# A two-layer graph kernel on one core: W_lang is loaded first, in four transfers, and TensorE's first product stands ahead of layer 0

## The reference, cut to what matters

```python
x = _layernorm(x + _L0_gnn_ref(x, adj, adj, L0_gnn_bias), axis=-1)
x = _layernorm(x + _L1_gnn_ref(x, adj, W_lang, W_grav, W_V, W_O, gate_logit, log_sigma), axis=-1)

# L0: W = adj * adj; out = einsum('bnf,nm->bmf', x, W) + bias
# L1:
z_l = einsum('bnd,ed->bne', h, W_lang); z_g = einsum('bnd,ed->bne', h, W_grav)
v = einsum('bnd,ed->bne', h, W_V)
zn = z_l / max(norm(z_l), EPS)
A_l = max(zn @ zn.T, 0) * not_eye
A_g = exp(-d2(z_g) / (2 sigma^2)) * not_eye
K = w_l * rows_normalised(A_l * adj) + (1 - w_l) * rows_normalised(A_g * adj)
out = (K @ v) @ W_O.T
```

## Time and profile before

| | us |
|---|---|
| median of 3 runs (lowest, highest) | 684.94 (684.61, 684.97) |
| the profiled execution, whole | 685.29 |
| its span, from first to last instruction | 683.5 |
| PE busy | 669.0 (98%) |
| PEld busy | 571.0 (84%) |
| DVE busy | 532.2 (78%) |
| ACT busy | 345.6 (51%) |
| POOL busy | 210.4 (31%) |

### The profile page before, as it was taken

The page is one execution under the profiler, slowest core; times in us unless marked ns, Lnnn a source line. Parts: engine busy times, 40 slices in busy tenths (PEclk is TensorE's granted clock), DMA queues, the critical chain, the costliest instruction groups (busy, mean ns, idle before and its releaser), DMA issues.

```text
span 683.5 us, 11745 instructions
## 1 busy us (share of the span) xinstructions
PE 669.0 (98%) x3579; PEld 571.0 (84%) x3579; DVE 532.2 (78%) x1523; ACT 345.6 (51%) x614; POOL 210.4 (31%) x454
## 2 busy tenths in 40 slices
PE   7999999999999999999999999999999999999994
PEld 6888888888888888888888888888888888888883
DVE  5935697878879787887968787796978779697786
ACT  4734445464454546455454645545474554545433
POOL 0222315051341515134151513416051331503022
PEclk9999999999999999999999999999999999999998
DMA  7201102011110201111020111102011110001002
GB/s 280 107 7 57 61 32 94 1 62 63 56 68 31 92 0 61 61 61 61 31 92 0 64 59 61 61 31 92 0 66 57 61 61 31 32 0 63 1 31 94
DMA packets 20406, 38.33 MB, mean 56 GB/s; under 512 B 1824, under 2 KB 1824, under 8 KB 20384
## 3 DMA queue, kind: packets, MB, share of 16 engines
q1 hardware_dynamic: 20384, 38.05, 15.3%
HBM read 21.27 MB, written 16.78 MB: 56 GB/s over the span
## 4 chain that ended last, share of the span: by engine, by line
PE 92%; DVE 3%; ACT 2%; DMA 1%; issue 1%; POOL 1%; SPq 0%; POOLq 0%; DVEq 0%
PE ring L357 56%; PE bank_p L377 12%; PE ring L475 4%; PE bank_x L318 3%; PE bank_p L318 3%; PE bank_k L421 3%; PE bank_r L421 3%; PE bank_pt L390 2%; PE bank_r L397 1%; DMA w_raw<-in_L_gnn_W_lang_dram 1%; PE bank_pt L336 1%; PE bank_r L336 1%; PE bank_k L336 1%; PE bank_pt L408 1%; PE bank_x L336 1%
## 5 line engine op out<-in xcount | busy, mean ns | idle before, releaser
L562 ACT ACTIVATE yT_hi<-ring 128x512 fp32r<-128x512 f32 x128 | 75.9, 593 | 113.5 <-PE ring L357 113.3
L357 PE MATMUL ring<-hT_hi,T_hi 128*128 128x512 f32 x320 | 130.5, 408 | 0.6 <-DVE hT_lo L772 0.5
L357 PE MATMUL ring<-hT_hi,T_lo 128*128 128x512 f32 x320 | 125.4, 392 | 0.0
L357 PE MATMUL ring<-hT_lo,T_hi 128*128 128x512 f32 x320 | 124.7, 390 | 0.0
L777 DVE TENSOR_TENSOR yT_lo<-ring,yT_hi 128x512 fp32r<-128x512 f32 x128 | 87.5, 684 | 35.3 <-ACT yT_hi L562 35.3
L357 PE MATMUL ring<-M_hi,hT_hi 128*128 128x512 f32 x256 | 101.5, 396 | 0.0
L357 PE MATMUL ring<-M_hi,hT_lo 128*128 128x512 f32 x256 | 100.2, 391 | 0.0
L357 PE MATMUL ring<-M_lo,hT_hi 128*128 128x512 f32 x256 | 99.9, 390 | 0.0
L1084 POOL TENSOR_SCALAR z_ve<-z_mv 128x2 f32<-128x2 f32 x32 | 7.0, 218 | 268.8 <-DVE z_mv L873 264.1
L1077 POOL TENSOR_TENSOR x_lo<-x_sb,x_hi 128x512 fp32r<-128x512 f32 x60 | 76.4, 1301 | 22.4 <-ACT x_hi L562 22.4
L614 ACT ACTIVATE o_sb<-o_sb,z_nb,z_rs 128x512 f32<-128x512 f32 x60 | 47.2, 810 | 62.3 <-POOL z_nb L1089 62.3
(11 more groups left out here) (159 smaller groups left out, 1390.6 us busy)
## 6 DMA issues: line engine op xcount, KB each, us to landing
x_sb<-in_x_dram SPq DMA_DIRECT2D x15, 1024.0 KB, 5.2
out_dram<-o_sb SPq DMA_DIRECT2D x60, 256.0 KB, 2.0
x_sb<-in_x_dram SPq DMA_DIRECT2D x2, 512.0 KB, 5.5
w_raw<-in_L_gnn_W_lang_dram SPq DMA_DIRECT2D x1, 1024.0 KB, 6.7
o_sb<-in_L_gnn_W_grav_dram SPq DMA_DIRECT2D x1, 1024.0 KB, 9.4
h_sb<-in_L_gnn_W_V_dram SPq DMA_DIRECT2D x1, 1024.0 KB, 11.6
w_raw<-in_L_gnn_W_O_dram SPq DMA_DIRECT2D x1, 1024.0 KB, 7.9
out_dram<-x_sb SPq DMA_DIRECT2D x4, 256.0 KB, 2.0
```

What stands on the lines that cost most here:

```text
L357: last = pe.matmul(bank[:, :], a, b, start=n == 0, stop=n == len(terms) - 1)
L562: return act.activation(dst, src, ACT.Copy, scale=scale)
```

## The change

SP loads W_lang first, in four DMAs of 128 rows with a semaphore each; adj, all of x (two DMAs), bias, gates, W_grav and W_V follow. TensorE does 21 warm-up transposes in place of 27; its block rows of L come first, then layer 0 of pairs 0 and 1, then row 0 of G, layer 0 of pairs 2 and 3, and rows 1 to 3 of G. ACT splits W_lang ahead of all of x, and its `hi_row`s and `hi_weight`s are put in another order. DVE splits W_lang ahead of the mix and takes out L row 0 ahead of splitting x.

```diff
-    WARM_UP = 27
+    WARM_UP = 21
+        w0_loaded = [sem(f"w0_loaded{c}") for c in range(DC)]
...
-            sp.dma_start(x_sb[:, 0:2, :], x_v[0][:, 0:2, :]).then_inc(x0_loaded[0], 16)
+            for c in range(DC):
+                sp.dma_start(w_raw[0][:, c, :], w_lang[c * R:(c + 1) * R, :]).then_inc(w0_loaded[c], 16)
             sp.wait_ge(adj_zeroed, 1)
             for b in range(2):
                 s = slice(b * N, (b + 1) * N)
                 sp.dma_start(adj_bd[s, s], adj).then_inc(adj_loaded, 16)
-            sp.dma_start(w_raw[0][:, :, :], w_lang.rearrange("(c p) d -> p c d", p=R)).then_inc(w_loaded[0], 16)
+            for c in range(2):
+                s = slice(2 * c, 2 * c + 2)
+                sp.dma_start(x_sb[:, s, :], x_v[0][:, s, :]).then_inc(x0_loaded[c], 16)
             sp.dma_start(bias_bc[:, :], bias.partition_broadcast(R)).then_inc(bias_loaded, 16)
-            sp.dma_start(x_sb[:, 2:4, :], x_v[0][:, 2:4, :]).then_inc(x0_loaded[1], 16)
...
-            pe.wait_ge(mix_steps, 5)
             for s in (L, G):
-                layer0(0, 2 * s)
-                layer0(0, 2 * s + 1)
                 for i in range(DC):
                     setup(...)
+                    if s == G and i == 0:
+                        layer0(0, 2)
+                        layer0(0, 3)
+                if s == L:
+                    pe.wait_ge(mix_steps, 5)
+                    layer0(0, 0)
+                    layer0(0, 1)
...
             def hi_weight(i):
-                act.wait_ge(w_loaded[i], 16)
+                if i:
+                    act.wait_ge(w_loaded[i], 16)
                 for c in range(DC):
+                    if i == 0:
+                        act.wait_ge(w0_loaded[c], 16)
...
+            hi_weight(0)
             split_x0(0)
-            hi_weight(0)
             split_x0(1)
 
             act.wait_ge(gates_loaded, 32)
...
             hi_row(L, 0)
+            hi_row(L, 1)
             hi_weight(1)
-            for i in range(1, DC):
-                hi_row(L, i)
+            hi_row(L, 2)
+            hi_row(L, 3)
+            hi_weight(2)
+            hi_row(G, 0)
             normalise_h(0, 0, 0)
             normalise_h(0, 0, 1)
-            hi_weight(2)
-            for i in range(DC):
-                hi_row(G, i)
-                if i >= 2:
-                    normalise_h(0, 0, i)
+            hi_row(G, 1)
+            hi_row(G, 2)
+            hi_row(G, 3)
+            normalise_h(0, 0, 2)
+            normalise_h(0, 0, 3)
...
-            dve.wait_ge(adj_loaded, 32)
-            (the four operations of mix)
...
-            split_x0(0)
-            dve.tensor_tensor(mask[:, :], adj_bd[:, :], off_diag[:, :], ALU.mult).then_inc(mix_steps, 1)
             lo_weight(0, 0, DC)
+            dve.wait_ge(adj_loaded, 32)
+            (the four operations of mix)
+            lo_row(L, 0)
+            split_x0(0)
+            lo_row(L, 1)
+            lo_weight(1, 0, DC)
+            lo_row(L, 2)
             split_x0(1)
             dve.wait_ge(bias_loaded, 16)
             add_y(0, 0, 0)
-            lo_row(L, 0)
+            lo_row(L, 3)
+            dve.tensor_tensor(mask[:, :], adj_bd[:, :], off_diag[:, :], ALU.mult).then_inc(mix_steps, 1)
             count_y(0, 0, 0)
-            lo_weight(1, 0, 2)
-            lo_row(L, 1)
-            lo_weight(1, 2, DC)
-            lo_row(L, 2)
-            lo_row(L, 3)
 
             dve.wait_ge(gate_exp, 1)
...
             dve.wait_ge(gate_steps, 3)
+            lo_row(G, 0)
             add_y(0, 0, 1)
             count_y(0, 0, 1)
             for i in range(DC):
-                lo_row(G, i)
+                if i:
+                    lo_row(G, i)
                 lo_weight(2, i, i + 1)
```

More of the change, by code:

```diff
@@ L966, in split_x0 @@
                     dve.tensor_tensor(x_lo[:, p, :], x_sb[:, p, :], x_hi[:, p, :], ALU.subtract).then_inc(x_lo_done, 1)
+            lo_weight(0, 0, DC)
+            dve.wait_ge(adj_loaded, 32)
+            dve.tensor_tensor(mix[:, :], adj_bd[:, :], adj_bd[:, :], ALU.mult).then_inc(mix_steps, 1)
+            dve.wait_ge(mix_steps, 2)
+            dve.tensor_tensor(mix[:, :], mix[:, :], ident[:, :], ALU.add).then_inc(mix_steps, 1)
+            dve.wait_ge(mix_steps, 3)
+            dve.tensor_copy(mix_hi[:, :], mix[:, :]).then_inc(mix_steps, 1)
+            dve.wait_ge(mix_steps, 4)
+            dve.tensor_tensor(mix_lo[:, :], mix[:, :], mix_hi[:, :], ALU.subtract).then_inc(mix_steps, 1)
+            lo_row(L, 0)
             split_x0(0)
-            dve.tensor_tensor(mask[:, :], adj_bd[:, :], off_diag[:, :], ALU.mult).then_inc(mix_steps, 1)
-            lo_weight(0, 0, DC)
+            lo_row(L, 1)
+            lo_weight(1, 0, DC)
+            lo_row(L, 2)
             split_x0(1)
```

## The result

The changed kernel takes 689.35 us (median of six executions, 687.95 to 1120.89) against 684.91 (684.61 to 685.16): the ratio is 1.0059, 95% interval 1.0045 to 1.0073. One execution, the 1120.89, had TensorE at a mean clock of 0.557 and is left out of the ratio; the other five lie between 687.95 and 689.87, with a median of 689.22. The profiled execution took 689.22 with a span of 687.4, 3.9 above the 685.29 of before.

A forecast was written before the change was run, and what follows sets the result against it. TensorE was taken to bound the kernel, with DVE's list, held by the gates' landing, deciding the setup; a 2.0 us shift on 684.94 gave 686.9 us, range 685.6 to 688.3.

The forecast's parts named there:

- DVE's list: DVE's setup work: idle from about 8.2 to about 13 us, then dense for 17.8 us to about 30.8.
- D0: The time DVE goes on after waiting for ACT's L row 0: 0.95 us after the gates land, 12.95.
- G - 10.0: Shift of the setup's end, where G is the gates' landing time in us; 2.0 us later for G = 12.0.
- the wait of pairs 2 and 3: PE idles about 1 us ahead of layer 0 of pairs 2 and 3, waiting for DVE's add_y.
- ACT waits for the second gate transfer for over 2 us: Sign expected in the changed profile: ACT stalls ahead of its exponentials until 11.4 to 12.7 us.
- I take the middle, G = 12.0: Gates' landing time, taken between 11.4 (whole queue hole gone) and 12.6 us (none of it gone).
- the hole: DMA queue at 121 in place of 408 GB/s from 3.50 to 5.00 us; 1.1 us lost, ramp 0.1 more.
- the low stretch: DMA queue at 84 GB/s from 9.50 to 11.00 us, put down to the gate transfers and expected to stay.
- The three more issues on SP take some 0.5 us each, but everything they issue is still queued behind data: SP's extra DMA issues for the split W_lang, some 0.5 us each, claimed to cost nothing.
- Rival B: Three extra W_lang transfer boundaries cost 0.45 us each; gates at 13.3, shift 3.3, time 688.2 us; chance 0.17.
- Rival D: TensorE's clock halves after a new idle hole, during G row 0; 1.2 us above forecast, 688.1; chance 0.03.
- C: DVE's wait is short: gates landing before 10.0 us make the kernel faster, 683.3 us; chance 0.04.

The follow-up runs named there:

- halves: The changed kernel with W_lang loaded in two transfers of 512 KB; 687.34 us.
- one_w_late: The changed kernel with W_lang in one transfer and SP waiting ahead of adj for TensorE's fourth warm-up transpose; 688.50 us.
- adj_act: The changed kernel with the two adj transfers issued by ACT on its own queue, so SP's x follows W_lang; 689.19 us.
- chunks_old: The kernel before with W_lang in four transfers of 256 KB in its old place, ACT waiting chunk by chunk; 685.11 us, ratio 1.0004.
- gates_act: The changed kernel with the two gate transfers issued by ACT as its first instructions instead of by SP; 688.90 us.
- after_again: The changed kernel measured once more, unedited; 688.47 us.
- exp_late: The changed kernel with ACT's gates wait and two exponentials moved behind hi_row(L, 0) and hi_row(L, 1); 689.35 us.

## Why the prediction was wrong

The direction, the mechanism and the chain were right; the time, 689.35 against a range up to 688.3, was not.

- "DVE's list": held. DVE idles from 8.7 to 14.9 and then takes 17.3 us to 32.2 (forecast 17.8 from D0).
- "G - 10.0": held within 0.15 us in seven of the nine executions of the table; in halves and one_w_late the measured shift is 0.5 and 0.7 us above it, for a reason given below.
- PE: held. Start at 6.05 (5.8), waits ahead of L row 3 and of the W_O transposes. Only the wait of pairs 2 and 3 was absent, as PE came there late itself (22.87).
- The sign "ACT waits for the second gate transfer for over 2 us" was not met, though the gates were later than forecast: the wait was 1.63 us, since x was late too and ACT split its second half only from 11.23.
- **The step that failed is the term "I take the middle, G = 12.0"**: the gates landed at 14.01 in the profiled execution, and at 14.30 and 11.84 in two more of the same program. Three parts of the term are wrong, and the cause behind them is open in part.
  - It treats the landing of one execution as a fixed quantity from which a hole is subtracted; one and the same program gives 11.8 to 14.3. The 11.84 execution took 687.29, 2.0 above the 685.29 of before, what I had forecast.
  - It gives back half of the hole, and keeps the low stretch as it was ("is the gates' own, and stays"). Up to 9.0 us the queue moved 228 GB/s on average, 238 before, so nothing of the hole was won back there. From 11.0 to 13.5 it moved 208 GB/s, 355 before: the low stretch grew. By an estimate from these numbers, 0.6 of the missing 2.0 us is the half of the hole that was not won, and the other 1.4 the longer low stretch; what lengthened it is not known.
  - "The three more issues on SP take some 0.5 us each, but everything they issue is still queued behind data": this was taken to cost nothing. With one transfer, and the rest issued 1.6 us later, the median rose 1.1 us (one_w_late). But adj_act, with x issued earlier, gained nothing, so this part is borne out by one run and not by the other.
- Rival B (chunked transfers leave gaps), with a chance of 0.17, went the right way and not far enough: G = 13.3 and 688.2, measured 14.01 and 689.35. Its reason is not shown: four transfers do cost 1.9 us against one, but late issue explains 1.1 of that, and in their old place they cost nothing.
- The rule of the Trainium skill, "DMA: Bandwidth & Descriptors", "Rules for kernel authors" (at least 1 MiB per DMA for full bandwidth) points the same way as the 1.9 us that four quarters cost against one, but not as halves, which cost nothing here (687.34 against 687.44), nor as chunks_old (685.11 against 684.85). The prediction's estimate of 11 us from the section "Anatomy of one DMA" of that page of the Trainium skill, fixed costs one behind another, did not come true: ACT began the last pair of chunks at 5.56. That section of the Trainium skill gives its 2.0 us for transfers issued by GpSimd; these are issued by SP.
- Rival D happened, and cost nothing in the changed kernel's profiled execution. After PE's 3.09 us of idle the granted clock was half:

```profile
16.20:19.60 3.40, 3.40 (x14) 3.02 (x14) 3.40 (x8) 2.94 (x8) 0.00 (x0) 0.51 0.94 366
```

  PE was ahead of DVE there: it still had to wait 0.71 us for DVE at 29.98. In other executions half a clock fell on the W_O transposes. It cost nothing in gates_act and after_again, where the last four ran at full clock. In halves and one_w_late it reached them, and they took 1.12 and 1.11 us in place of 0.66:

```profile
31.71 1.12 PE L506 MATMUL ring<-ident,w_raw 128*128 128x128 f32 x4
```

```profile
33.07 1.11 PE L508 MATMUL ring<-ident,w_raw 128*128 128x128 f32 x4 [0.28 <-DVE hT_lo L1016]
```

  From their start to M's first row it is 2.39 and 2.61 us in place of 1.72. These 0.7 and 0.9 us are why the two shifts lie above the relation, so D is worth something after all in some executions.
- The other side, C, needed gates by 10.0. None of the executions of this transfer order came near it.

## What to carry to other kernels

When an engine's start is brought forward, ask what its partner engine waits for in order: here a 4-byte scalar at the end of a 2.3 MB queue held up the whole of DVE's list, and behind it stood the next transfer, so that removing the first wait alone gained nothing. Take what is needed late out of the head of the queue and out of the head of the list together. Take a transfer's landing from several executions, or give it a range as wide as they show: 2.5 us here.

## What the runs showed that I had not expected

The landing of a small transfer that stands eleventh in the queue varied by 2.5 us between executions of one program (11.84 to 14.30), and it carried straight into the kernel's time: the changed kernel's executions spread over 2.8 us (687.29 to 690.06) where those of before lie between 684.39 and 685.64 but for one at 687.15. Between the landing of x and that of the gates, 4 us passed in exp_late for 257 KB: the second half of x was split on ACT at 9.93, and the exponential started at 13.94.
